# A second attention layer's prologue issued inside the last batch of the gated layer ahead of it

## What is computed

```
x = x + _L0_ffn_ref(_layernorm(x), w_gate, w_up, w_down)      # f0: (silu(h w_gate) * (h w_up)) w_down, 1024 hidden
x = x + _L1_attn_ref(_layernorm(x), W_qkv, W_proj)            # a1: 16 heads of 16, causal softmax attention
```

## Time and profile before

| | |
|---|---|
| median of 3 runs | 1858.33 us (1858.04 to 1858.57) |
| span of the profiled execution | 1867.2 us |
| PE busy in it | 1647.8 us (88%) |
| DVE / ACT / POOL busy | 1131.8 / 867.8 / 470.7 us |
| DMA, mean share of 16 engines | 30.0% |

### The profile page before, as it was taken

How to read it: one execution, slowest core, us unless ns; L and a number is a source line. 1 busy time by engine, 2 the same in 40 slices (tenths; PEclk the granted TensorE clock), 3 DMA queues, 4 the chain that set the end, 5 groups by cost and what they waited for, 6 DMA issues and landing times. The chain is left out here.

```text
span 1867.2 us, 29072 instructions
## 1 busy us (share of the span) xinstructions
PE 1647.8 (88%) x10776; PEld 966.2 (52%) x10782; DVE 1131.8 (61%) x2567; ACT 867.8 (46%) x1358; POOL 470.7 (25%) x593
## 2 busy tenths in 40 slices
PE   4899999899999999954799999779998999998776
PEld 2344444478855666533456656456774344443533
DVE  2687777343245665647667776355454787774476
ACT  1266556533215555532135555447671566665322
POOL 4222120023313322010332230036772522200100
PEclk9799899999999999965899999979999999999699
DMA  7350441100064345000534532211114345320322
GB/s 243 88 142 35 108 119 23 68 1 0 1 175 128 85 120 159 2 9 0 155 93 129 142 114 47 77 52 52 52 52 139 99 105 158 88 71 1 122 91 91
DMA packets 68961, 160.30 MB, mean 86 GB/s; under 512 B 10285, under 2 KB 15926, under 8 KB 67962
## 3 DMA queue, kind: packets, MB, share of 16 engines
q1 hardware_dynamic: 68826, 158.51, 30.0%
HBM read 109.05 MB, written 53.09 MB: 87 GB/s over the span
## 5 line engine op out<-in xcount | busy, mean ns | idle before, releaser
L1078 DVE TENSOR_REDUCE a_mx<-PS 128x1 f32<-128x512 f32 (+3 forms) x768 | 395.0, 553 | 192.6 <-PE PS L1320 128.8
L1261 ACT ACTIVATE a_pT<-PS 128x1024 f32<-128x1024 f32 (+3 forms) x384 | 310.4, 812 | 214.8 <-PE PS L1344 151.7
L1315 PE MATMUL PS<-a_k,a_q 64*128 64x512 f32 (+3 forms) x768 | 231.9, 414 | 10.2 <-DVE a_mx L1078 6.1
L405 DVE CUSTOM_DVE_ANT_0 PS<-PS,a_dist 128x448 f32<-128x448 f32 x256 | 156.4, 644 | 62.9 <-PE PS L650 60.6
L1335 PE MATMUL PS<-a_q,a_k 64*128 64x512 f32 (+3 forms) x768 | 172.5, 435 | 6.8 <-issue 5.0
L1358 PE MATMUL PS<-a_pT,a_va 128*32 128x512 f32 (+3 forms) x1536 | 164.3, 499 | 5.6 <-ACT a_raw L1219 5.4
L555 ACT ACTIVATE a_pT<-PS 128x448 f32<-128x448 f32 (+1 forms) x256 | 124.6, 540 | 92.1 <-PE PS L673 91.8
L122 PE MATMUL PS<-cst 128*128 128x512 f32 x248 | 132.0, 661 | 37.7 <-PEq L66 28.7
L1315 PEld LDWEIGHTS PS<-a_k,a_q 64*128 64x128 f32 x768 | 110.1, 185 | 79.4 <-DVE a_mx L1078 60.7
L1335 PEld LDWEIGHTS PS<-a_q,a_k 64*128 64x128 f32 x768 | 74.9, 184 | 144.1 <-issue 68.5
L2074 POOL TENSOR_TENSOR f_h_low<-f_prod,f_h_high 128x512 fp32r<-128x512 f32 x84 | 111.5, 1334 | 60.8 <-ACT f_h_high L2261 55.6
(11 more groups left out here) (355 smaller groups left out, 3406.4 us busy)
## 6 DMA issues: line engine op xcount, KB each, us to landing
spread_scratch<-a_high SPq DMA_DIRECT2D x96, 256.0 KB, 3.4
a_q<-spread_scratch SPq DMA_DIRECT2D x96, 256.0 KB, 5.5
a_k<-spread_scratch SPq DMA_DIRECT2D x96, 256.0 KB, 6.2
f_gb<-gate_rows SPq DMA_DIRECT2D x68, 256.0 KB, 5.1
spread_scratch<-a_low SPq DMA_DIRECT2D x48, 256.0 KB, 4.1
a_q<-window_scratch SPq DMA_DIRECT2D x32, 256.0 KB, 5.4
a_k<-window_scratch SPq DMA_DIRECT2D x32, 256.0 KB, 6.0
window_scratch<-a_high SPq DMA_DIRECT2D x24, 256.0 KB, 4.7
```

Of the source, the lines that this page charges most:

```text
L405: dve.tensor_tensor_reduce(PS[:, 4 + a, 0:KW], PS[:, 4 + a, 0:KW], dt_[:, off:off + KW], 1.0, 3e38, ALU.add, ALU.min, mx[:, gg % 2, qt, 2 ...
L1078: dve.tensor_reduce(mx[:, gg % 2, qt, 2 * half + a:2 * half + a + 1], PS[:, 4 + a, 0:kw], AX.X, ALU.max).then_inc(max_done, 1)
L1261: act.activation(pT[:, N // 2 % 2, N % 2, :, q0:S], PS[:, 2 * (N % 2):2 * (N % 2) + 2, q0:S], ACT.Exp, scale=SCALE).then_inc(exp_done, 1)
L1315: mm = pe.matmul(ps[:, 0:kw], q[rows, b % 2, pair, qt * P:(qt + 1) * P], k[rows, b % 2, pair, 0:kw], start=True, stop=not causal)
```

## The change

The prologue of a1 is cut into steps (`norm`, `unit`, `values`, `scores`, ...) that each engine's program offers. `swiglu` gets a1's stage as `ahead` and issues these steps in its last batch, between its own instructions; a1's own block then consists of the load of `wo`, two memsets on POOL (`zeros`, and the second half of `va`) and the main loop. a2 and a3 run the same steps in their own blocks, as before, except for those two memsets, which move behind the prologue there too. The 28 `keep_busy` matmuls of a1 are gone. SBUF is now laid out by hand (`Ground`): a1's prologue buffers lie where f0 has none (a number behind a name in the rows below is only a buffer's), or over f0's raw weights `wi`. The weights for a1 are loaded into `va[0]`, the masks into `m`, right behind f0's own loads. The units use banks 0, 1, 6, 7 (before: 2, 3, 0, 1), the values banks 0 and 1, and f0's last output tile bank 0.

```diff
             def _(sp):
                 ...
                 sp.dma_start(wd[:, :], w_down[:, :]).then_inc(loaded_d, 16)
+                following = ahead.sync(sp)
+                following.load()
+                following.spread_batch(0)
             ...
+                following = ahead.pool(pool)
+                following.norm()
+                for n in range(NHT):
+                    lower(NB - 1, n)
+                    if n == 4:
+                        following.fill()
+                    if n == 5:
+                        following.norm_next()
+                following.split_maxima(0)
             ...
+                following = ahead.vector(dve)
+                following.norm_stats(0)
+                for n in range(NHT):
+                    hidden(NB - 1, n)
+                    if n == 0:
+                        following.norm_apply(0)
+                    elif n == 1:
+                        following.weights_low(0)
+                    elif n == 2:
+                        following.input_low()
+                    elif n == 3:
+                        following.weights_low(1)
+                        following.keep_unit(0)
+                        following.keep_unit(1)
                     ...
+                for t in range(TB):
+                    add_outputs(NB - 1, t, last_banks[t])
+                    for s in range(max(0, 8 * t - 4), min(24, 8 * t + 4)):
+                        following.maxima(s)
+                following.keep_maxima(0, 0)
             ...
+                following = ahead.scalar(act)
+                following.weights_high(0)
+                for n in range(NHT):
+                    hidden(NB - 1, n)
                     ...
+                    elif n == 6:
+                        following.keep_values(0, 0, ahead.value_banks[0])
+                        following.keep_values(0, 1, ahead.value_banks[1])
+                hidden_high(NB - 1, NHT - 1)
+                following.keep_maxima(0, 0)
             ...
+                following = ahead.tensor(pe)
+                begin(NB - 1)
+                for n in range(NHT):
+                    hidden(NB - 1, n)
+                    if n == 2:
+                        for c in range(KC):
+                            following.turn(0, c, c)
+                    elif n in (3, 4):
+                        following.unit(2 * n - 6)
+                        following.unit(2 * n - 5)
+                    elif n in (5, 6):
+                        following.values(n - 5)
+                following.units_kept()
+                for t in range(TB):
+                    if t == TB - 1:
+                        pe.wait_ge(ahead.va_done, 1)
+                    for n in range(NHT):
+                        down(NB - 1, t, n, last_banks[t])
+                        if t == 1 and n == 3:
+                            pe.wait_ge(ahead.masks_done, 1)
+                        if t and n % 4 == 3:
+                            for s in range(8 * t + n - 11, 8 * t + n - 7):
+                                following.scores(s)
+                following.turn_maxima(0, 0)
```

More of the change, by code:

```diff
@@ L48, with __init__, take, outside @@
 UMAX = 2 * S - P - GLOB
+SBUF_FIRST, SBUF_END = 35968, 229376
 class Names:
     pass
+class Ground:
+    def __init__(self, nc, tag, spans):
+        self.nc, self.tag, self.free, self.taken = nc, tag, [list(s) for s in spans], {}
+    def take(self, name, shape, dt=F32):
+        size = math.prod(shape[1:]) * (2 if dt == BF16 else 4)
+        size += -size % 32
+        span = next(s for s in self.free if s[1] - s[0] >= size)
+        self.taken[name] = (span[0], span[0] + size)
+        span[0] += size
+        return self.nc.alloc_sbuf_tensor_at(f"{self.tag}_{name}", shape, dt, offset=self.taken[name][0])
+    def outside(self, spans):
+        edges = sorted(self.taken.values())
+        left = []
+        for lo, hi in spans:
+            for a, b in edges:
+                if a < hi and b > lo:
+                    if a > lo:
+                        left.append((lo, a))
+                    lo = max(lo, b)
+            if lo < hi:
+                left.append((lo, hi))
+        return left
 @contextmanager
@@ L958, in fetch_group @@
[L958 to L971, removed]
@@ new lines, in spread_batch, with loop @@
+            def spread_batch(b):
+                store_unit(b, 0)
+                store_unit(b, 1)
+                fetch_group(b, 0)
+                fetch_group(b, 1)
+                store_unit(b, 2)
+                store_unit(b, 3)
+                fetch_group(b, 2)
+                fetch_group(b, 3)
+            def loop():
+                for b in range(1, NB):
+                    spread_batch(b)
+            p.load, p.load_last, p.spread_batch, p.loop = load, load_last, spread_batch, loop
@@ L1430, in _ @@
-                if causal:
-                    pe.wait_ge(masks_done, 1)
-                for t in range(4 * TB + 4):
-                    scores(t)
-                    if t % 2:
-                        keep_busy(pe, PS, cst, 3, 1)
-                pe.wait_ge(va_done, 2)
-                turn_maxima(0, 0)
-                for t in range(4 * TB + 4, LEAD):
-                    scores(t)
-                keep_busy(pe, PS, cst, 3, 3)
+                        pe.matmul(PS[:, 2 * half + a, q0:q0 + 64], half_masks[rows, 0, 0, :],
+                                  half_masks[rows, 2, 0, 0:64], start=False, stop=False)
@@ new lines, in piece @@
+            def piece(kind, b, i, before):
+                if kind == "none":
+                    return
+                for done, value in freed(before) if before else ():
+                    pe.wait_ge(done, value)
+                if kind == "maxima":
+                    turn_maxima(b, i)
+                elif kind == "group":
+                    turn_group(b, i)
+                elif kind == "turn":
+                    turn(b, i, 7)
+                elif kind == "project":
+                    project(b, i, 7)
+                elif kind == "values":
+                    values_of(b, i, 7)
+                elif kind == "heads":
+                    turn_heads(b, i)
+                else:
+                    outputs(b, i)
@@ L1452, in _ @@
                 before = previous_piece(FULL)
-                for p in LAST:
-                    piece(*p, before if bank_of(*p) == 7 else None)
+                for last in LAST:
+                    piece(*last, before if bank_of(*last) == 7 else None)
                 for done, value in freed(LAST[-1]):
                     pe.wait_ge(done, value)
-def swiglu(nc, tag, X, cst, PS, w_in, w_down):
+            p.turn, p.unit, p.values, p.scores, p.turn_maxima = turn, first_unit, first_values, scores, turn_maxima
```

1052 lines of the change are left out of this document (593 added, 459 removed).

## The result

The changed kernel takes 1844.27 us (median of 7 runs, 1837.56 to 1853.46) against 1858.57 for the kernel before in 7 runs beside it (1857.54 to 1866.49): a ratio of 0.9921, 95% interval 0.9895 to 0.9947. It is faster, as forecast, but by 14.3 us instead of 22.2, and it lies outside the range. Over all runs of this study the kernel before has a mean of 1858.4 us (105 runs, error 0.5) and the changed one 1846.9 (37 runs, error 0.9): a gain of 11.5 us. (The four times that both ran beside each other give 14.7, 16.6, 8.7 and 10.1 us by the means.) The first question is whether the stretch that the sum was made for came out as summed. First the page's first line and two windows: from PE's first matmul of f0's last batch to its first of a1's loop, and the loop's start (the earlier trace rows for before).

The account below looks back on a forecast made before the run. PE alone was taken to bound f0's last batch, while filler hid a serial chain in a1's prologue. PE's terms summed to 60.3 us against 82.65, a gain of 22.3, so 1858.33 became 1836.1 us; range 1832 to 1843.5.

Parts of the forecast that it names:

- The sum: PE's real work from f0's last batch to a1's loop: 60.3 us against 82.65, gain 22.3; chance 0.77.
- hidden blocks, turn, units and values: PE in f0's last batch: eight blocks 22.4 us, norm's turn 1.0, four units 5.67, values 2.84.
- the first score tile: Before it in f0's last batch, PE waits 1.8 us for `f_h_low`, among output tiles of 2.83 us each.
- six runs of score tiles: 24 score tiles in f0's last batch: 12.5 us, with 2.5 us per run of 512 columns.
- tail: End of f0's last batch: last maxima, DVE's copy of 1.23 us and the barrier of 0.88, together 2.8 us.
- What is put at nothing: Costs taken as 0: spread, loads, ACT's copies, moved memsets; in a3 0.4 us might show, in a2 POOL waits for DVE.
- The clock: At the border of f0 and a1: a gap of about 2.2 us leaves the clock at 1.00, cost nothing.
- Rival (a): Clock falls once at the barrier or score tiles: 10 us at half costs up to 5 us, 1841 us; chance 0.11.
- Rivals (b) to (e): Score tiles cost 19.2 us (0.06); spread late (0.03); slower, clock stays half (0.03); no gain, prologue already hidden (excluded).
- The base: Kernel before: traced span 1867.2 us, median 0.5% below it, 1858.33; the gain was subtracted from these.

Follow-up runs that it names:

- e4: Changed kernel with three filler matmuls added at the border of f0 and a1 (label matched by elimination): 1850.85 us (12 runs).
- e5: Label not tied to a run in the text; by order probably the changed kernel with POOL waiting for DVE's norm before the two memsets: 1839.53 us.

## Why the prediction missed

- **The sum, held.** Point by point from the changed kernel's trace: hidden blocks, turn, units and values from 473.04 to 504.75, 31.7 us (forecast 31.9); from there to the first score tile 5.9 (6.05, with PE's wait for POOL in it); six runs of score tiles and the output matmuls between them 20.5 (19.6); tail 3.2 (2.8). DVE's norm came just ahead of the eighth product, without harm. The miss here is 0.95 us, mostly at the score tiles: a run of 512 columns takes 2.7 us, not 2.5. (Two figures of the working are off in the last digit and carry nothing: 1829.5 should be 1829.6, and 519.8 + 0.42 is 520.22, where the trace has 520.26.)
- **The failed step** is in "What is put at nothing": "2.2 - 1.8 = 0.4 us may show [...] I take 0 and keep 0.4", and for a2 "POOL waits for DVE behind the memset". I asked who waits for POOL, and the answer, nobody in these prologues, was right: a third memset didn't lengthen them. I didn't ask who runs beside it. The price was in the trace of before: in f3 one of DVE's four norm operations took 1.87 us beside the memset (2.83 for the four, shown above), against 1.37 us for four without one. By that row a norm operation that starts beside 2.3 us of memsets lasts until their end, about 2.1 us in each of a2 and a3. With the clock's falls behind them, as measured, it is 4.9 and 5.7 us.
- **The clock.** "I take nothing" for the border was wrong on the clock and nearly right on the time, the second by luck: the low price of a fall was nowhere in the reasoning. Rival (a) came true, 10.2 us at half, and not by chance: in all eleven traces with the stop of 2.5 us the clock is at half behind it, in the two where filler cuts it to 1.22 us it isn't. (The stop isn't needed for it: in two of four traces with a1's filled prologue as before it fell 5.3 us into the loop.) The price of 5 us was wrong: it cost about 1, since PE is busy only 8.1 of 10.65 us there. I had read 98.05 of 100 us from the loop's middle and used it for its start. The same size of fall behind the stop in a3's prologue cost more: 5.7 us less the stop's own 2.1 leave some 3.5, and where only 3.4 us were at half behind the same stop (`e4`) the prologue took 53.6 us instead of 55.5. There filler stands between the score tiles and stretches too, 2.08 us for two matmuls instead of 1.12. The rule of the Trainium skill that I weighed, page "TensorE: Matmul & The Clock Gate", section "HAM oscillation — how this bites in real kernels", names the level that came; its example is a longer wait, for a DMA, so that a stop of 2.5 us is no clean test of it. What a fall costs only the busy share of the very stretch tells.
- **Rivals (b) to (e)** fell: a run of four tiles takes 1.6 to 2.7 us, so 13.4 for the 24, not 19.2; no fetch was waited for; nothing stayed at half.
- **The base.** 1867.2 us was no typical execution: its a0 and f0 took 485.2 us up to the last batch, where 18 traces range from 473.9 to 485.7. The median of three runs with a spread of 0.5 us looked exact; 105 runs spread from 1847.7 to 1869.6, and that it lies at their mean is luck. The range of 3 us either way was too narrow for that alone.
- **In sum**, 22.2 us forecast: 1 lost in the sum, 5.5 (by the times) to 10.6 (by the traces) to the memsets, the rest to falls of the clock in untouched code and to chance. The version with the memsets back, 1841.4 us over 29 runs, beats both kernels.

## What to carry to other kernels

When a step moves on POOL, look at what DVE runs beside its new place, not only at who waits for POOL; a DVE operation that is longer than its like in the trace is the sign, and a wait of POOL for DVE costs less than the overlap. Price a fall of the clock by PE's busy share in that very stretch at full clock. Take the spread of executions from many runs, or compare untouched stages of two traces, before a range of a few us is given.

## What was unexpected of the hardware

A POOL instruction can hold a DVE operation from SBUF to SBUF until it ends: a norm operation took 2.51 us instead of 0.40 beside two memsets of 0.52 and 1.80, and 1.87 beside one of 1.80. Two memsets back to back held it through both; where POOL waited in between, it got in. Very short POOL operations held nothing that shows: beside the splits of the maxima (16 columns, 0.25 to 0.37 us) norm operations took their 0.41. A memset isn't needed: a subtraction of DVE with both inputs in SBUF took 2.33 us instead of 1.23 beside POOL's remainder in f0's last batch (POOL, then DVE; slack covered it):

```profile
480.09 1.29 POOL L1688 TENSOR_TENSOR f_h_low<-f_hid,f_h_high 128x512 fp32r<-128x512 f32 x1 [4.26 <-ACT f_h_high L1785]
480.13 2.33 DVE L1218 TENSOR_TENSOR a_w_lowqk<-a_va,a_w_highqk 128x1024 fp32r<-128x1024 f32 x1
```

Two kinds weren't held: maxima that read PSUM (0.64 us each beside the memsets), and that same subtraction beside a memset. In the kernel before it took its 1.23 us beside the memset of 3.52:

```profile
526.41 1.23 DVE L1134 TENSOR_TENSOR a_w_lowqk<-a_pT,a_w_highqk 128x1024 fp32r<-128x1024 f32 x1 [0.56 <-ACT a_w_highqk L1234]
```

That memset starts 0.39 us behind the subtraction, which by itself would prove little; in a2 the subtraction starts 0.88 us behind the memset's start and takes 1.22 us too. So it depends on both sides: the norm was held by memsets and, in f0 of the kernel before, by a remainder (2.38 us for its four operations), the subtraction only by a remainder, which reads SBUF. The Trainium skill, page "SBUF — State Buffer", section "Who interferes with whom", has the rule: some DVE forms and GpSimd share a pair of ports, whoever comes first keeps it for the whole instruction, and the other is blocked, not slowed; with two inputs in SBUF a DVE instruction collides only with a GpSimd one that reads. The traces agree on the kinds and on the block: in f3 and f0 POOL's instruction starts 0.08 and 0.04 us ahead and DVE is held. They show the reverse as well. In f2 DVE's subtraction `f_lat_low` and POOL's remainder start within 0.02 us of each other; in the changed kernel's trace POOL's takes 1.83 us instead of 1.29 and DVE's its 0.68, in that of `e5` DVE's takes 1.83 and POOL's 1.30. In a2 and a3 the rows don't settle who came first: DVE's operation starts 0.11 us ahead of the memset in them, 0.08 of it under the operation before. That the hold can run on through a second POOL instruction is the traces' own: 2.51 us beside two memsets.
